# Masking the turned softmax weights on ScalarE instead of GpSimd, between the staging of rows and the projection's copies

## The reference

```python
def attn(x):                                        # b=4, s=1024, h=16, d=16
    Q, K, V = [(x @ W.T).reshape(b, s, h, d) for W in (Wq, Wk, Wv)]
    scores = einsum('bshd,bstd->bsht', Q, K) / sqrt(d)
    return einsum('bsht,bstd->bshd', softmax(scores, -1), V).reshape(b, s, dm) @ Wfc.T
x = layernorm(x + attn(x))
topk_idx, topk_w = route(x)                         # 4 of 32 experts
mixed = (expert_out[topk_idx] * topk_w).sum(1)      # down(silu(gate x) * up x), I = 128
shared = (silu(x @ Wsg.T) * (x @ Wsu.T)) @ Wsd.T
x = layernorm(x + mixed + shared)
```

## Time and profile before

| | |
|---|---|
| time, median of 3 runs | 704.72 us (700.75 to 709.49) |
| profiled execution | 712.17 us, span 710.6 us |
| mean granted TensorE clock | 0.914 |
| busy: TensorE, VectorE, ScalarE, GpSimd | 583.4, 389.8, 241.0, 346.9 us |
| masking on GpSimd (L439) | 32 instructions, 49.8 us |
| steps 4 to 7 of the first stage | about 37 to 39 us each, from 108 to 260 us |

### The profile page before, as it was taken

One profiled execution on the slowest core, in us unless ns is written; L12 is line 12 of the kernel. 1 busy time (PEld: TensorE's weight loads), 2 busy tenths in 40 slices (PEclk: granted clock), 3 DMA queues, 4 the chain that ended last, 5 costly groups with the idle time before them and its releaser, 6 DMA issues.

```text
span 710.6 us, 16465 instructions
## 1 busy us (share of the span) xinstructions
PE 583.4 (82%) x4916; PEld 452.5 (64%) x4917; DVE 389.8 (55%) x1285; ACT 241.0 (34%) x490; POOL 346.9 (49%) x346
## 2 busy tenths in 40 slices
PE   6954799999999997978740199999999999993993
PEld 2541648475757666665530198888988889882873
DVE  2160538474858667647480056655655655561864
ACT  2312133325151614233120044554545545440224
POOL 4051302656565655745647336655565565552121
PEclk9978899999999999778795599999999999996998
DMA  6948491939584799286317444555555555445995
GB/s 226 232 124 222 133 236 45 266 117 261 159 239 151 218 305 327 102 307 235 129 68 248 141 124 142 151 154 156 151 145 147 152 157 156 150 122 181 419 411 211
DMA packets 124956, 135.34 MB, mean 190 GB/s; under 512 B 77288, under 2 KB 105967, under 8 KB 124272
## 3 DMA queue, kind: packets, MB, share of 16 engines
q1 hardware_dynamic: 105424, 92.95, 45.5%
q0 software_dynamic: 13248, 35.72, 13.3%
q10 hardware_dynamic: 6240, 6.09, 2.5%
HBM read 74.79 MB, written 60.96 MB: 191 GB/s over the span
## 4 chain that ended last, share of the span: by engine, by line
PE 62%; DMA 10%; DVE 9%; issue 8%; ACT 3%; SPq 3%; DVEq 2%; POOLq 1%; POOL 1%; ACTq 0%
PE bank L631 57%; DMA wgu_sb<-pick_rows 3%; PE bank L790 3%; DMA prod<-expert_rows 2%; DVEq L241 1%; DVE prod L1120 1%; ACT prod L547 1%; DMA q_slots<-wd_sb 1%; DVE prod L1144 1%; DMA pick_rows<-prod,ids 1%; SPq L376 1%; POOL expert_rows L448 1%; POOLq L248 1%; PE bank L732 1%; DMA k_slots<-wd_sb 1%
## 5 line engine op out<-in xcount | busy, mean ns | idle before, releaser
L470 POOL DMA_INDIRECT pick_rows<-prod,ids x136 | 137.0, 1007 | 110.7 <-issue 51.3
L448 POOL DMA_INDIRECT expert_rows<-stage,pos x128 | 127.4, 996 | 64.0 <-issue 38.4
L631 PE MATMUL bank<-prod 128*128 128x128 f32 x1088 | 137.3, 280 | 8.7 <-issue 5.3
L631 PEld LDWEIGHTS bank<-prod 128*128 128x128 f32 x1088 | 128.2, 194 | 15.5 <-issue 8.5
L439 POOL TENSOR_SCALAR wgu_sb<-wgu_sb,t_mask 128x512 f32<-128x512 f32 x32 | 49.8, 1566 | 121.1 <-DVE wgu_sb L912 121.1
L631 PE MATMUL bank<-wd_sb,wqkv_sb 128*128 128x512 f32 x192 | 87.0, 611 | 7.0 <-DMA wqkv_sb<-in_wqkv 6.2
L1120 DVE COPY prod<-wgu_sb 128x512 f32 x136 | 57.8, 466 | 61.1 <-issue 46.1
L631 PE MATMUL bank<-wgu_sb 128*32 128x64 f32 x2048 | 63.3, 296 | 22.6 <-issue 13.8
L631 PEld LDWEIGHTS bank<-wgu_sb 128*32 128x32 f32 x2048 | 60.1, 137 | 29.7 <-issue 29.7
L790 PE MATMUL bank<-ident,prod 128*128 128x128 f32 x272 | 42.5, 280 | 37.5 <-DMA prod<-expert_rows 37.2
L590 ACT ACTIVATE prod<-bank,kept 128x256 f32<-128x256 f32 x136 | 57.0, 470 | 42.3 <-PE bank L631 30.9
(11 more groups left out here) (136 smaller groups left out, 790.3 us busy)
## 6 DMA issues: line engine op xcount, KB each, us to landing
prod<-expert_rows SPq DMA_DIRECT2D x136, 132.0 KB
wgu_sb<-pick_rows SPq DMA_DIRECT2D x32, 512.0 KB, 14.1
wgu_sb<-in_wgu SPq DMA_DIRECT2D x2, 2560.0 KB, 12.6
wd_sb<-in_xT SPq DMA_DIRECT2D x8, 512.0 KB, 4.1
q_slots<-wd_sb SPq DMA_DIRECT2D x16, 256.0 KB, 4.3
k_slots<-wd_sb SPq DMA_DIRECT2D x16, 256.0 KB
wgu_sb<-q_slots SPq DMA_DIRECT2D x16, 256.0 KB, 4.1
wgu_sb<-k_slots SPq DMA_DIRECT2D x64, 64.0 KB
```

The source lines that it names most:

```text
L448: pool.indirect_dma_start(xs, bass.IndirectOffsetOnAxis(ap=pos[:, i, k:k + 1], axis=0), stage[:, i, k, :], None, bounds_check=XROWS - 1, o ...
L470: pool.indirect_dma_start(z, bass.IndirectOffsetOnAxis(ap=ids[par][:, j:j + 1], axis=0), y_sb[par][:, j, :], None, bounds_check=TOPK * NTO ...
L631: return pe.matmul(dst, lhsT, rhs, start=(k == 0), stop=(k == n - 1))
```

## The change

The masking moves from GpSimd's queue to ScalarE's. There it stands between `stage_rows(e)` and `evacuate(a)`, as four activations (Copy with the mask as a per-partition scale) in place of four tensor_scalar multiplications. Its waits are the same: for PT, and for the weighted sum that read the PTx before. ScalarE waits for the masks once, at its start, and GpSimd no longer does.

```diff
 @block.gpsimd
-            pool.wait_ge(S["masks"], 4)
...
-            def expand(p, hf):
-                pool.wait_ge(S["pT"], 2 * p + hf + 1)
-                if p:
-                    pool.wait_ge(S["o_ready"], 2 * p - 1 + hf)
-                for t2 in range(QB):
-                    pool.tensor_scalar(PTx[:, hf, :, t2 * NH:(t2 + 1) * NH],
-                                       PT[:, hf, :].rearrange("p (i m) -> p i m", m=NH),
-                                       t2_mask[:, t2:t2 + 1], None, ALU.mult).then_inc(S["ptx_ready"], 1)
...
             for s in range(CH + 4):
-                p, b, e = s - 1, s - 3, s - 4
-                if chunk(p):
-                    for hf in range(HALF):
-                        expand(p, hf)
+                b, e = s - 3, s - 4
                 if chunk(b):
                     invert(b)
...
 @block.scalar
             act.wait_ge(S["consts"], NCONST)
+            act.wait_ge(S["masks"], 4)
...
+            def expand(p, hf):
+                act.wait_ge(S["pT"], 2 * p + hf + 1)
+                if p:
+                    act.wait_ge(S["o_ready"], 2 * p - 1 + hf)
+                for t2 in range(QB):
+                    act.activation(PTx[:, hf, :, t2 * NH:(t2 + 1) * NH],
+                                   PT[:, hf, :].rearrange("p (i m) -> p i m", m=NH),
+                                   ACT.Copy, scale=t2_mask[:, t2:t2 + 1]).then_inc(S["ptx_ready"], 1)
...
                 if chunk(e):
                     stage_rows(e)
+                if chunk(p):
+                    for hf in range(HALF):
+                        expand(p, hf)
                 if chunk(a) and s != 1:
                     evacuate(a)
```

## The result

| | before | after |
|---|---|---|
| median of 20 runs each | 707.74 us (700.75 to 711.21) | 712.59 us (708.14 to 719.8) |
| ratio | | 1.0085, 95% interval 1.0062 to 1.0107 |
| profiled execution's span | 710.6 us | 709.4 us |
| busy GpSimd / ScalarE | 346.9 / 241.0 us | 296.1 / 259.1 us |

The change costs 0.85%, 6.0 us (4.4 to 7.6) on 707.74. The ratio and its interval leave out two executions of the changed kernel that ran at a lower granted clock (719.36 and 719.8 us), and they are not the quotient of the two medians, which lie 4.85 us apart. With 20 runs the median of before is 3 us above that of the first three, so the forecast of 710.3 us is best read as its ratio, 1.008.

The account below looks back on a forecast made before the run. TensorE, busy 82% of the span, was taken to bound the attention loop's steps 4 to 7. Terms 3.9 + 0.3 − 0.3 + 1.7 = +5.6 us on the 704.72 us median gave 710.3 us, range 703.5 to 718 us.

Parts of the forecast that it names:

- GpSimd's work is worth nothing: Removing 32 maskings, 49.8 us of GpSimd, gains 0: about 19.5 us of slack, and nobody waits for this engine.
- 0.70 us a masking, 2.4 us for the four: Price on ScalarE: 0.70 us for one masking alone, 0.60 us in a row, 2.4 us for a step's four.
- Rival 1: Maskings on ScalarE cost like `copy_o` or GpSimd's own: +13.2 us (717.9 us) or +24 us (729 us); chance 0.09.
- TensorE stands still for 1.0 us: Before the projection's third product in steps 4 to 7, waiting for ScalarE's first copy: 4 x 0.97, +3.9 us.
- 0.31 + 1.12 = 1.43 us: ScalarE's idle around its first projection copy in step 6, taken as cover for the 2.4 us inserted.
- Step 2, +0.3 us: Third product about 2 us late, off the path; SyncE's write of K moves from 60.22 to 60.5 us.
- vepst, −0.3 us: VectorE's small add takes 0.17 us instead of 0.43 without GpSimd masking beside it; on the chain only in step 8.
- The clock, +1.7 us: One more fall of TensorE's granted clock in steps 4 to 7, 1.7 us each; ends −3.4 and +6.8 us.
- Rival 2: TensorE's clock falls in each of the four projections: +10.7 us, 715.4 us; chance 0.13.
- Rival 3: Clock falls in steps 4 and 7 go away: +0.5 us, 705.2 us; includes cheaper maskings, +2.4 us; chance 0.18.
- rival 4: GpSimd is on the path after all and scatters start earlier: −1 us, 703.7 us; chance 0.03.

Follow-up runs that it names:

- e8_pool_six: The kernel before with six maskings instead of four on GpSimd, the extra ones into memory nobody reads; ratio to before 0.9965.
- e1: The changed kernel with each masking behind one of the projection's first four copies, on a chip where before takes 816 us; ratio to before 1.0044.
- f2: The changed kernel with each masking behind one of the projection's first four copies, on a chip where before takes 709 us; ratio to before 1.0017.
- e6: The changed kernel with the second half of each chunk masked on GpSimd, the first on ScalarE; ratio to before 0.9982.
- e7: The changed kernel with all maskings at the end of ScalarE's step; ratio to before 1.0023.
- f4: The changed kernel with six maskings instead of four ahead of the copies, on a chip where before takes 709 us; ratio to before 1.0211.
- f1: The changed kernel run again without edits, on a chip where before takes 709 us; ratio to before 1.0122.
- f3: The changed kernel with ScalarE masking in steps 4 to 7 only, GpSimd in the others, where before takes 709 us; ratio to before 1.0047.
- e4_six: The changed kernel with six maskings instead of four ahead of the copies, on a chip where before takes 816 us; ratio to before 1.0291.

## Why the prediction was right

- **GpSimd's work is worth nothing** ("Worth 0"): shown, by the idle of 14.28 and 2.76 us after and by e8_pool_six.
- **0.70 us a masking, 2.4 us for the four:** 0.706 and 2.45. Rival 1, dear writes, is out. The Trainium skill's 93 ns for a pointer operand ("ScalarE: Activation LUTs", What ACT_TABLE_LOAD costs) is met by 706 − 620 = 86 ns, and its note in "SBUF — State Buffer" (Door 1: The DMA port swizzle) by 706 ns for runs of 64 bytes against 1063 ns for `copy_o` in the same trace.
- **"TensorE stands still for 1.0 us":** right in its place and mechanism, which e1/f2, e6 and e7 show by taking it away and f4 by more than doubling the gap with two more maskings. The term was too small: 4 x 0.97 = 3.9 us is the gap between records, the step grew by 1.24 us, so 5.0 us. The step that failed is the cover, "0.31 + 1.12 = 1.43 us", read from ScalarE's idle with the copy of bank 1 at 203.53 us taken as the moment "when TensorE moves on to the third product". TensorE moved on at 203.25 us, and the cover is about 1.15 us.
- **Step 2, +0.3 us:** the stall came (2.19 us, said: about 2). K's write starts 1.3 us later than in the earlier trace rows, not 0.3, behind a Q write whose issue took 3.00 us instead of 1.31:

```profile
58.47 3.00 SPq L272 DMA_DIRECT2D q_slots<-wd_sb  x2
61.51 2.65 SPq L272 DMA_DIRECT2D k_slots<-wd_sb  x2
```

  The scores start no later for it. The term is lost in the spread of the transfers.
- **vepst, −0.3 us:** 0.17 us as said, but not for the reason given, by e8_pool_six; too small to be told in a time.
- **The clock, +1.7 us:** direction plausible, not shown. Counting gates of about 8.8 us in steps 3 to 7, the three traces with a gap of about 1 us in steps 4 to 7 (after, f1, f3) have 1, 3 and 2 falls, those without one (before, f2, e6, e7, e8) have 2, 2, 1, 0 and 0. The gates are not all of it: the clock also falls behind `weigh`'s pause in step 6 of f2 (0.50 from 194 to 196 us) and e6, and in step 8 of after. Rival 2, a fall in each projection, did not happen at a 1 us gap (7.13 us in all of after, f1 and f3); at 2.2 us it happened in three of four. That was the right rival for a larger dose.
- **Rival 3, not slower,** is out by the interval, rival 4 by GpSimd's wait for `pos`.

5.0 us of stall account for the 6.0 us measured within its interval (4.4 to 7.6); f1_after's 1.0122, 8.7 us, is 3.7 above them, at an interval of 4.9 to 12.3. What lies between stays open. The traces say where to look: f1_after's execution is 9.5 us longer than that of after, and of these 3.1 us lie ahead of step 4, 0.3 us in steps 4 to 7 and 6.1 us in steps 8 to 10, at a lower granted clock.

That the sum of 5.6 us came so near to the 6.0 measured is in part luck. The stall was 1.1 us larger than its term, the 1.7 us for the clock and the 0.3 us for step 2 were not seen, and these errors partly cancel. No version beat the kernel before clearly: e6_half and f2_between, which place the same work well, hold 1.00.

## What to carry to other kernels

An engine's idle share does not make it a cheap host: ask where in its queue the work would stand, what waits behind it, and how long the queue has before its next release is due. Here 2.4 us in front of the first of six copies cost 1.2 us a step, and the same work dealt out between the copies left no gap and no cost that the times could show. Measure the cover from the waiting engine's own pace (when its third product would start), not from the idle of the engine that serves it; and don't expect a gain from unloading an engine that nobody waits for.

## What the runs showed that was not expected

- A gap in TensorE's row understates the stall: 0.98 us of gap, 1.24 us of step.
- TensorE's granted clock fell behind a 2.2 us gap in three of four projections of f4_six (1.7 us each), behind gaps of 2.17 to 2.61 us in two of four of e4_six, not behind the 2.19 us gap of step 2 in after, and never behind a 1.0 us gap in twelve; the falls behind the 0.79 us idle of `turn` came in some steps and not in others, also in kernels with no other gap.
- Two executions of the changed kernel differ by 9.5 us, more than the change costs, and 6.1 us of it lie in steps 8 to 10, which the change does not touch except for the maskings of step 8.
- The same program took 816 us on one chip and 709 us on another, with ScalarE held ahead of one activation for some 10 us a step.
